# Leaky unit of a graph kernel's first rounds: a ScalarE Relu and a scaled sum, with VectorE's steps through accumulator banks

## The reference

```python
def prop(z):
    return segment_sum(edge_weight[:, None] * z[src], dst, num_segments=50000)
for i in range(5):
    z = h @ W[i] + b[i]
    x_start = prop(z)
    xi = h
    for _ in range(5):
        xi = (prop(xi) + x_start) / 2.9
    mean, var = mean(xi, axis=0), var(xi, axis=0)
    out = gamma[i] * (xi - mean) / sqrt(var + 1e-5) + beta[i]
    h = where(out > 0, out, 0.01 * out)          # leaky unit
return h[seg_ids]
```

## Time and profile before

| | us |
|---|---|
| median of 3 runs (9603.39 to 9615.67) | 9612.27 |
| profiled execution, its own time | 9691.98 |
| span of the profiled execution | 9690.2 |
| POOL busy in the span | 6759.2 (70%) |
| PE busy | 5711.1 (59%) |
| DVE busy | 5407.2 (56%) |
| ACT busy | 1448.9 (15%) |

### The profile page before, as it was taken

How to read it: one execution, slowest core, us unless ns; L and a number is a source line. 1 busy time by engine, 2 the same in 40 slices (tenths; PEclk the granted TensorE clock), 3 DMA queues, 4 the chain that set the end, 5 groups by cost and what they waited for, 6 DMA issues and landing times. The chain is left out here.

```text
span 9690.2 us, 103316 instructions
## 1 busy us (share of the span) xinstructions
PE 5711.1 (59%) x24229; PEld 4276.2 (44%) x24229; DVE 5407.2 (56%) x12873; ACT 1448.9 (15%) x3028; POOL 6759.2 (70%) x6509
## 2 busy tenths in 40 slices
PE   4646557766666766666666666666661775630191
PEld 2436224544444544444545445544440664530170
DVE  5668764554445754456744457644457774530277
ACT  0115000210002200012200012100026113430006
POOL 4767663577777777777777777777776776767566
PEclk8765776775555855556855557755555888865555
DMA  3137101577555765656678656668766227961107
GB/s 144 43 101 245 25 3 36 118 111 99 98 98 103 132 104 98 98 98 112 124 99 101 99 97 124 113 98 96 99 99 232 63 68 149 183 115 28 20 31 323
DMA packets 564282, 1024.03 MB, mean 106 GB/s; under 512 B 192219, under 2 KB 275724, under 8 KB 563556
## 3 DMA queue, kind: packets, MB, share of 16 engines
q0 software_dynamic: 192032, 330.29, 32.3%
q1 hardware_dynamic: 354372, 588.76, 20.1%
q10 hardware_dynamic: 17664, 102.61, 2.6%
HBM read 561.87 MB, written 471.67 MB: 107 GB/s over the span
## 5 line engine op out<-in xcount | busy, mean ns | idle before, releaser
L1018 POOL DMA_INDIRECT G<-tab,gidx x4000 | 4050.6, 1013 | 1625.4 <-issue 1406.8
L1347 PE MATMUL PS<-M,G 128*128 128x128 f32 x6400 | 2073.2, 468 | 1524.1 <-DVE M L1382 1011.7
L1347 PEld LDWEIGHTS PS<-M,G 128*128 128x128 f32 x6400 | 1504.5, 314 | 2175.3 <-DVE M L1382 917.5
L1410 DVE TENSOR_TENSOR_SCAN UO<-keyrow,UT,PS 128x512 f32<-128x512 f32 (+1 forms) x400 | 511.9, 1280 | 1112.9 <-PE PS L1347 1112.9
L1410 DVE TENSOR_TENSOR_SCAN UT<-keyrow,UO,PS 128x512 f32<-128x512 f32 (+1 forms) x400 | 512.0, 1280 | 1030.7 <-PE PS L1347 1030.7
L1326 ACT COPY big<-UO 128x512 f32 (+1 forms) x100 | 61.8, 618 | 3666.0 <-DVE UO L1410 3666.0
L1434 DVE TENSOR_TENSOR Y<-PS,big 128x512 f32<-128x512 f32 x800 | 546.0, 683 | 12.8 <-PE PS L1372 7.0
L1105 POOL DMA_INDIRECT Y<-pair_d,G x400 | 402.4, 1006 | 200.0 <-issue 130.8
L1382 DVE TENSOR_TENSOR M<-ident,wz 128x512 f32<-128x512 f32 x800 | 534.3, 668 | 0.0
L758 ACT ACTIVATE big<-big,nb,rs 128x128 f32<-128x128 f32 x1173 | 461.3, 480 | 428.0 <-POOL nb L749 357.7
L1372 PE MATMUL PS<-ident,UT 128*128 128x128 f32 x1600 | 422.8, 420 | 8.3 <-DVE UT L1410 8.3
(11 more groups left out here) (500 smaller groups left out, 11436.0 us busy)
## 6 DMA issues: line engine op xcount, KB each, us to landing
tab<-Y SPq DMA_DIRECT2D x1050, 256.0 KB, 3.2
big<-agg SPq DMA_DIRECT2D x90, 832.0 KB, 12.6
G<-tab,gidx POOLq DMA_INDIRECT x4000, 4.1
WR<-w_d SPq DMA_DIRECT2D x200, 256.0 KB
big<-x SPq DMA_DIRECT2D x60, 832.0 KB, 4.9
xt_d<-big SPq DMA_DIRECT2D x30, 858.0 KB, 19.2
x2n<-big ACTq DMA_DIRECT2D x30, 838.5 KB, 3.5
big<-x2n SPq DMA_DIRECT2D x30, 838.5 KB, 12.6
```

The source lines that it names most:

```text
L1018: pool.indirect_dma_start(G[:, t % RG, 0:D], None, tab_in(k), bass.IndirectOffsetOnAxis(ap=gidx[:, t:t + 1], axis=0)).then_inc(l_got[t % R ...
L1347: ins = nc.tensor.matmul(PS[:, FT_[h], j, :], G[:, s, 0:D], M[:, GR * h + j, :], start=True, stop=True)
L1410: nc.vector.tensor_tensor_scan(S[h], keyrow[:, bass.ds(tile * P, GR * P)], half if k == 0 else bank(FT_[h]), S[1 - h][:, GR * P - 1:GR * P ...
```

## The change

The leaky unit max(0.01 y, y) of y = s x + t is written as Relu(0.99 s x + 0.99 t) + (0.01 s) x + 0.01 t. ACT computes the first term (Relu for Identity, with `lk[:, 0:2]` as scale and bias), and DVE adds (0.01 s) x with a scalar_tensor_tensor that takes `lk[:, 2:3]` as a pointer scalar.

- Kept rows: ACT writes its Relu into bank ZB instead of `HT` or `OT`; DVE adds `zt` scaled to it and writes `HT` or `OT`. The constant 0.01 t is left out there, and comes in through `bias_z` = bias + (0.01 t) W, computed once per layer by one more PE product and one more addition.
- Gathered rows: ACT writes into `M` as before; DVE adds bank FT scaled to it, into new banks V (6 and 7). The product with `WR` adds 0.01 t first and works in place in bank V; the scan reads bank V.
- The addition into `zt` moves from behind the scan to in front of it, and takes `bias_z`.
- ACT's wait on `l_z` becomes one on `l_za`; DVE's `leaky_nodes` gets a wait on `l_z`.

```diff
@@ layer-wide names
+        lk = sb("lk", [P, 4])
+        bias_z = sb("bias_z", [P, D])
-        FT_, BK_, ZB_ = (0, 1), (2, 3), (4, 5)
+        FT_, BK_, ZB_, V_ = (0, 1), (2, 3), (4, 5), (6, 7)
@@ -1309,13 +1311,13 @@
             for i, q in every_group(act):
                 h, n, g = q % 2, (l - 1) * GPR + NB * i + q, group_no(l, 0, i, q)
                 steady(act, n + 1, g + 3, g + 1)
-                act.wait_ge(l_z, n + 1)
-                nc.scalar.activation(HTR[h][:].rearrange("p s f -> p (s f)"), zt_at((NB * i + q) * GR), ACT.Identity,
-                                     bias=tcol[:, 0:1], scale=scol[:, 0:1]).then_inc(l_hc, 1)
+                act.wait_ge(l_za, n + 1)
+                nc.scalar.activation(bank(ZB_[h]), zt_at((NB * i + q) * GR), ACT.Relu,
+                                     bias=lk[:, 1:2], scale=lk[:, 0:1]).then_inc(l_hc, 1)
                 act.wait_ge(l_ft, g + 3)
                 act.wait_ge(l_sc, g + 1)
-                nc.scalar.activation(M[:, GR * h:GR * h + GR, :], PS[:, FT_[h], :, :], ACT.Identity,
-                                     bias=tcol[:, 0:1], scale=scol[:, 0:1]).then_inc(l_he, 1)
+                nc.scalar.activation(M[:, GR * h:GR * h + GR, :], PS[:, FT_[h], :, :], ACT.Relu,
+                                     bias=lk[:, 1:2], scale=lk[:, 0:1]).then_inc(l_he, 1)
 
         def kept_act(act, l):
 
@@ -1384,9 +1386,12 @@
                                         ALU.mult).then_inc(l_dg, 1)
 
             def leaky_nodes(i, q):
-                u, n = HTR[q % 2][:].rearrange("p s f -> p (s f)"), (l - 1) * GPR + NB * i + q
+                n = (l - 1) * GPR + NB * i + q
                 dve.wait_ge(l_hc, n + 1)
-                nc.vector.scalar_tensor_tensor(u, u, 0.01, u, ALU.mult, ALU.max).then_inc(l_hl, 1)
+                dve.wait_ge(l_z, n + 1)
+                nc.vector.scalar_tensor_tensor(HTR[q % 2][:].rearrange("p s f -> p (s f)"),
+                                               zt_at((NB * i + q) * GR), lk[:, 2:3], bank(ZB_[q % 2]),
+                                               ALU.mult, ALU.add).then_inc(l_hl, 1)
 
             def scanned(i, q):
                 h, g, tile = q % 2, group_no(l, k, i, q), (NB * i + q) * GR
@@ -1394,12 +1399,17 @@
                 half = M[:, GR * h:GR * h + GR, :].rearrange("p s f -> p (s f)")
                 if k == 0:
                     dve.wait_ge(l_he, n + 1)
-                    nc.vector.scalar_tensor_tensor(half, half, 0.01, half, ALU.mult, ALU.max).then_inc(l_lr, 1)
+                    nc.vector.scalar_tensor_tensor(bank(V_[h]), bank(FT_[h]), lk[:, 2:3], half, ALU.mult,
+                                                   ALU.add).then_inc(l_lr, 1)
                     if not is_last(i, q):
                         leaky_nodes(i + (q + 1) // NB, (q + 1) % NB)
                     dve.wait_ge(l_lr, n + 1)
                     dve.wait_ge(l_wc[q % NG], 32 * (NB // NG * NI * (l - 1) + NB // NG * i + q // NG + 1))
-                    nc.vector.tensor_tensor(half, half, WR[:, q % NG, :], ALU.mult).then_inc(l_mu, 1)
+                    nc.vector.scalar_tensor_tensor(bank(V_[h]), bank(V_[h]), lk[:, 3:4], WR[:, q % NG, :], ALU.add,
+                                                   ALU.mult).then_inc(l_mu, 1)
+                    dve.wait_ge(l_z, n + 3)
+                    nc.vector.tensor_tensor(zt_at(tile).rearrange("p (s f) -> p s f", f=D), PS[:, ZB_[h], :, :],
+                                            wide(bias_z, P, GR), ALU.add).then_inc(l_za, 1)
                     dve.wait_ge(l_mu, n + 1)
                 else:
                     dve.wait_ge(l_ft, g + 3)
@@ -1408,13 +1418,9 @@
                 if last:
                     dve.wait_ge(l_zc, n + 1)
                 nc.vector.tensor_tensor_scan(S[h], keyrow[:, bass.ds(tile * P, GR * P)],
-                                             half if k == 0 else bank(FT_[h]), S[1 - h][:, GR * P - 1:GR * P],
+                                             bank(V_[h] if k == 0 else FT_[h]), S[1 - h][:, GR * P - 1:GR * P],
                                              ALU.mult, ALU.add).then_inc(l_sc, 1)
-                if k == 0:
-                    dve.wait_ge(l_z, n + 3)
-                    nc.vector.tensor_tensor(zt_at(tile).rearrange("p (s f) -> p s f", f=D), PS[:, ZB_[h], :, :],
-                                            wide(bias, P, GR), ALU.add).then_inc(l_za, 1)
-                elif not is_last(i, q):
+                if k and not is_last(i, q):
                     scaled_identity(i + (q + 1) // NB, (q + 1) % NB)
                 if last:
                     dve.wait_ge(l_sc, g + 3)
@@ -1454,7 +1460,7 @@
             dve.wait_ge(l_bn2, 3 * (l - 1) + 3)
             nc.vector.tensor_scalar(col[:, 1:2], col[:, 4:5], float(POS) / N, None, ALU.mult).then_inc(l_st, 1)
 
-        NCOEF = 6
+        NCOEF = 7
 
         def inverse_deviation(pool, l):
             steady(pool, NCOEF * (l - 1) + 3)
@@ -1478,6 +1484,11 @@
             dve.wait_ge(l_col, v + 5)
             nc.vector.tensor_tensor(tcol[:], gb[:, 1, bass.ds(l - 1, 1)], col[:, 2:3], ALU.subtract).then_inc(l_col, 1)
             dve.wait_ge(l_col, v + 6)
+            nc.vector.tensor_scalar(lk[:, 0:1], scol[:], 0.99, None, ALU.mult)
+            nc.vector.tensor_scalar(lk[:, 1:2], tcol[:], 0.99, None, ALU.mult)
+            nc.vector.tensor_scalar(lk[:, 2:3], scol[:], 0.01, None, ALU.mult)
+            nc.vector.tensor_scalar(lk[:, 3:4], tcol[:], 0.01, None, ALU.mult).then_inc(l_col, 1)
+            dve.wait_ge(l_col, v + 7)
 
         def over_layers(eng, program):
 
@@ -1564,7 +1575,11 @@
                         dve.wait_ge(l_w, 32 * l + 32)
                         nc.vector.tensor_tensor(BD.rearrange("p (s f) -> p s f", f=D), wide(bias, P, GR),
                                                 ident[:, 0:GR].unsqueeze(2).to_broadcast([P, GR, D]), ALU.mult)
+                        nc.vector.tensor_scalar(HT[:, 0, :], ones[:], lk[:, 3:4], None, ALU.mult)
                         nc.vector.tensor_tensor(wplus[:], wmat[:], ident[:], ALU.add).then_inc(l_wr, 1)
+                        dve.wait_ge(l_bz, l)
+                        nc.vector.tensor_tensor(bias_z[:], PS[:, BK_[1], 0, :], bias[:], ALU.add).then_inc(l_bv, 1)
+                        dve.wait_ge(l_bv, l)
                         for k in range(NL):
                             l1_dve(dve, l, k)
                         totals(dve, l)
@@ -1605,6 +1620,8 @@
                         return
                     steady(pe, l)
                     pe.wait_ge(l_wr, l)
+                    pe.wait_ge(l_ev, round_of(l, 0) * GPR + 2)
+                    nc.tensor.matmul(PS[:, BK_[1], 0, :], HT[:, 0, :], wmat[:], start=True, stop=True).then_inc(l_bz, 1)
                     for k in range(NL):
                         l1_pe(pe, l, k)
                 over_layers(pe, layer)
```

More of the change, by code:

```diff
@@ L920, in build @@
         l_g0 = pool_sems("l_g0", 1)[0]
-        l_w, l_wr, l_base, l_m, l_rows, l_keep, l_pad, l_first = (
-            sem("l_" + n) for n in "w wr base m rows keep pad first".split())
+        l_w, l_wr, l_base, l_m, l_rows, l_keep, l_pad, l_first, l_bz, l_bv = (
+            sem("l_" + n) for n in "w wr base m rows keep pad first bz bv".split())
         l_ft, l_sc, l_bk, l_ev, l_dg, l_he, l_mu, l_lr, l_hl, l_hc, l_z, l_za, l_zc, l_xc, l_mk, l_bn, l_bn2, l_st, l_col, l_pw = (
```

## The result

| | before | after |
|---|---|---|
| median of 20 runs, us | 9609.62 | 9591.51 |
| profiled execution, own time | 9691.98 | 9586.8 |
| POOL busy | 6759.2 | 6575.1 |

The ratio is 0.9983, 95% interval 0.9976 to 0.9989. Faster, but by 18 us, outside the forecast's range (9453 to 9560) and just under the 19 us that the forecast had set as what can be told.

What follows compares the result with a forecast made beforehand. POOL's gathers, lengthened beside DVE steps with two SBUF inputs, were taken to bound rounds k = 0. Savings of 144 - 2.4 - 8 = 134 us off the 9612 us median gave 9478 us, range 9453 to 9560.

Steps and rivals of the forecast that it cites:

- What bounds the kernel: Rounds k = 0: POOL sets the pace, 5.72 us a group, its gathers lengthened beside DVE steps with two SBUF inputs.
- Inputs moved to banks: DVE's steady steps in rounds k = 0: no two SBUF inputs, so gathers take 0.95 us, saving 144 us in four rounds.
- Does DVE keep up: DVE's six steps per group in rounds k = 0: 4.35 us, 0.65 under POOL's 5.0; writing a bank costs nothing extra.
- The addition in front: Addition into `zt` before the scan: covered by DVE's room except in each round's last group, 2.4 us lost in all.
- ACT: ACT's two passes per group, one now into a bank, and its new wait for an earlier addition: cost 0.
- the start of a layer: Extra small instructions and a PE product at layer start, some 2 us, hidden behind PE's wait for rows: cost 0.
- What is late next: Transfers in rounds k = 0 at 5.0 us a group: DMA share 0.78 to 0.84, 8 us lost in all.
- the ring: Buffer for gathered groups between POOL and PE: holds five groups, 25 us, so even landings of 7.0 us are swallowed.
- The turn stays: From a round's last gather start to the next round's first pass: stays 14.8 us, but for 0.6 us.
- The partial rival: DVE, PE or transfers hold rounds k = 0 near 5.3 us a group: saving 74 us, time 9538, chance 0.14.
- The forecast's sign of being wrong: Gathers shrink but rounds k = 0 don't: POOL then waits for PE, and the length of steps into banks tells which case.

Runs made afterwards that it cites:

- row_before: Kernel before the change, with `WR` loaded into only one partition from the sixth group of a round k = 0 on: 9554.01 us, ratio 0.9993.
- pe_row: Changed kernel with PE making the weight rows from one fp32 row instead of the broadcast load, nothing left out: 9431.15 us, ratio 0.9855.
- best_row: pe_row plus, in rounds k > 0, the scaled identity made from a copy of `ident` in a bank: 9414.05 us, ratio 0.9828.
- scan_m3: Changed kernel with one move undone: the product writes `M` and the scan reads `M` in SBUF again: 9517.56 us, ratio 0.9942.
- add_behind: pe_row with the addition into `zt` put back behind the scan: 9438.53 us, ratio 0.9856.
- row_after: Changed kernel with `WR` loaded into only one partition from the sixth group of a round k = 0 on: 9422.89 us, ratio 0.9853.
- half_round: Changed kernel with full `WR` loads for groups 5 to 24 of each round k = 0, one partition for the rest: 9471.47 us, ratio 0.9885.
- pe_weights: Changed kernel with PE making the weight rows from three bf16 parts in bank V, nothing left out: 9472.11 us, ratio 0.9891.
- again: The kernel before the change, run once more unaltered for a second trace: 9565.16 us in a single run.
- half_after: Changed kernel with `WR` loaded into 64 of 128 partitions after the first five groups of a round k = 0: 9494.35 us, ratio 0.9916.
- best: pe_weights plus, in rounds k > 0, the scaled identity made from a copy of `ident` in bank V: 9433.82 us, ratio 0.9854.
- row3_w3: row3_after with the three rows read from pe_weights' table `w3_d`, without its product: 9476.22 us, ratio 0.9892.
- row3_after: Changed kernel with three 1 KB pieces from another table than pe_weights' loaded in place of `WR`, no PE weight product: 9433.29 us, single run.

## Why the prediction was wrong

By its own steps:

- **What bounds the kernel: right.** row_before shows POOL as the bound, with gathers of 1.10 to 1.13 us on average and the transfers at a share of 0.42 to 0.43.
- **Inputs moved to banks: right.** 190.5, 191.1, 188.9, 189.2 us of gathers for 190 forecast. The inference in the Trainium skill, "SBUF — State Buffer", "Who interferes with whom", that `tensor_tensor` doesn't hold up descriptor making does not agree with these runs for the indirect gathers here: beside the scaled identity, a `tensor_tensor` with two SBUF inputs, they take up to 1.46 us in pe_row, and none over 0.97 in best_row, where one input lies in a bank. The mean gather of rounds k = 0 fell from 1.13 to 0.95 us when DVE's pairs of SBUF inputs went, and scan_m3, with the scan alone put back, has 1.05 to 1.07. The section's other sentence, that a VectorE instruction with two SBUF inputs contends with a GpSimd instruction that reads SBUF, agrees: a gather takes its positions `gidx` from there. Which part of a gather is held was not told apart.
- **Does DVE keep up: right.** Its steps took 0.74 to 0.75, 0.68, 0.67 and 1.27 us; writing a bank cost nothing, at the lower end taken. In backlog, at the end of the first round, a group took 4.34 us for 4.35.
- **The addition in front, ACT, the start of a layer: right** within what can be told (1.1 us for 2.4 by add_behind).
- **"What is late next": this step failed.** It said that at a pace of 5.0 us the DMA share would be 0.78 to 0.84, that a landing of even 7.0 us is "swallowed" by the ring, and took off 2 us a round, at most 15. Measured: rounds of 293.7 us on average where 265.4 were due with nothing taken off, so 28 us a round instead of 2, some 10 of them in the turn. It scaled the share by the rate, as if a packet's time were fixed. Row_after and the change have nearly the same gather packets, and 0.23 against 0.46 us for each. Once the share neared 1, landings of 14 us and stores of 22 us followed. The ring does swallow most of the gathers' delay (half_round, pe_weights: hardly a wait within the rounds); what it can't swallow is DVE's wait for `WR`, with no such ring and loads issued behind a store, and the turn, which waits for the last store.
- **"The turn stays": wrong** by the same cause, 22 to 31 us for 14.8.

The partial rival, 5.3 us a group, came near the pace (from its first to its last gather a round took 5.3 to 5.5 us a group) and named the transfers, but it was argued and priced by DVE and PE alone and left the turn as it was: 9538 us, 53 too few. The forecast's sign of being wrong came as written: gathers shrank, rounds didn't, and POOL waited for PE, but behind it stood the transfers and not the steps into banks. A warning was in the trace before: landings of 7.0 us at k = 1, where fewer bytes flow than at k = 0 with 4.8. A round whose landings lengthen with fewer bytes is no matter of bytes. The window of that round shows it plainly (the kernel before, layer 1, k = 1 and k = 4; then the same rounds k = 0 and 1 in the second trace, again):

```profile
2062.05:2329.00 266.95, 196.06 (x200) 0.51 0.84 98
2863.00:3135.00 272.00, 201.44 (x200) 0.51 0.56 96
```

```profile
1759.00:2058.00 299.00, 225.93 (x200) 0.84 0.67 133
2058.00:2320.00 262.00, 191.62 (x200) 0.51 0.50 100
```

A share of 0.84 and one of 0.56, at 98 and 96 GB/s, and 0.50 for the 0.84 in the other execution of the same kernel, with landings of 3.4 us. So the slowness is not bound to the change: it also came in some rounds of one execution of the kernel before. I read the share as load, with room from 0.73 to 1; it was partly slowness already.

What stays open: what tips the transfers into congestion. Shown are three facts. More bytes and a quicker pace bring it (change, half_after), a slower pace with the full bytes does not (scan_m3), and it can outlast the bytes by 80 us and more (half_round). It also comes at low bytes in all three kernels with the table `w3_d` (pe_weights, best, row3_w3: 4 KB packets of 0.86 to 0.95 us over rounds k = 0). The like ones without it have 0.45 to 0.68, but 0.78 in the first round of add_behind, and none of them has a turn over 15.2 us. That gathers outstanding in numbers slow each other down is my reading of half_round, and no run took their number alone as its variable.

## What to carry to other kernels

Before a gather stream is made quicker, read packets, MB and share of its queue in several windows: if the share moves without the bytes, a packet's time is not fixed, and shares must not be scaled by the rate. Look at who waits for the other transfers beside that queue, loads without a deep ring and the stores that a turn waits for. Here the change alone gave 0.9983 and the loads cut alone 0.9993 (row_before), but the change with one row and a product on PE in place of the 256 KB broadcast loads 0.9855, and with the identity in a bank 0.9828.

## What the runs showed of the hardware

- Congestion of the indirect gathers: some 1000 packets of 2 MB in 40 us take 37 and 47% of the engines' time in two kernels (row_after, row3_after) and 71 and 78% in two others (the change, row3_w3). In half_round it lasted 80 us and more after the broadcast loads had stopped.
- A kernel with longer gathers (scan_m3, 1.05 to 1.07 us) is (0.9983 - 0.9942) x 9610 = 39 us faster than the change, which issues them in 0.95.
- A `tensor_tensor` of VectorE with both inputs in SBUF lengthens gathers beside it, to 1.46 us at most (pe_row, k = 1 to 3 of layer 1); with one input in a bank none of 600 passes 0.97 (best_row).
- A step of VectorE with a pointer scalar that reads a bank takes 0.75 us for 128 x 512 when it writes a bank, in place or another, and 0.74 when it writes SBUF: the bank as destination costs nothing.
- A product 1 x 128 by 1 x 512 on TensorE for each group replaced a 256 KB broadcast with rounds of 264 to 266 us, as with no weights made at all (row_after).
